# A routed feed-forward with LoRA conditioning, attention pooling and a quantised feed-forward: the first gather moved into the routing stage, slots and weights in a table of their own, copies of x spread, pooling loads moved up

## The chip, the cores and the metric

The kernel runs on one core of one Trainium2 chip. A core has TensorE (PE) for matmuls, VectorE (DVE), ScalarE (ACT) and GpSimd (POOL) for elementwise work, and SyncE (SP), which here only issues transfers. Each engine runs its own instruction stream, and they meet through semaphores. SP's transfers and POOL's run on the same 16 DMA engines, from two queues (q1 and q0 in the profile). The metric is the device time of one execution in microseconds, the median of several runs. One further execution is taken with the hardware profiler; all rows below are of that one.

## The reference

Eight batches of 512 tokens, 512 features, 4096 tokens in all. Cut to what matters:

```python
# stage 1: conditioning and routing. The experts see only the conditioned tensor c.
c = (x @ A[lang].T) @ B[lang].T + emb[lang]          # rank 16, 4 languages
vals, idx = top_k(c @ E.T, 2)                        # 8 experts, softmax over the two
caw = weights * (cumsum(weights > 0, axis=0) <= 512) # each expert keeps its first 512 tokens
tokens = c[index]                                    # 512 rows for each expert
out = relu(tokens @ w1[e].T) @ w2[e].T * vals        # inner width 1024
x = x + zeros.at[index].add(out)                     # scatter-add
# stage 2: attention pooling of x, then a feed-forward 512 -> 2048 -> 512 with
# row-quantised inputs (int8) and ternary weights, added to x
scores = tanh(x @ W1 + b1) @ v ; p = softmax(where(mask, scores, -1e30))
pooled = (p @ x) / count
out = x + bitlinear(gelu(bitlinear(pooled, w1, b1)), w2, b2)
```

c is never formed. It has rank 68 (64 LoRA coordinates and 4 language flags), so a token is a short row of features, and the first product of each expert is taken with G = (B, emb)-transposed times w1[e].

## The kernel before, in words

The program is four blocks one after another, with a barrier of all engines between them. At a block's end every engine executes a DRAIN and signals POOL, which releases all.

**Block 1, routing.** SP issues the small inputs, eight loads of the transposed x (`xt`, a ring of three), `w_in` of experts 0 to 2 and `w_raw` of expert 0, and then eight copies of x, 1 MB each, from the input to the DRAM tensor `x_after_experts` (x1), into which the experts add. For each batch PE makes the features (`feats`) and turns them; ACT keeps them in `feat` (`feat_cp`). The 32 tiles of 128 tokens are routed in two halves q. `choose(q)` on DVE finds the two best experts; the softmax needs one exponential on ACT, `exps(q)`. PE counts (`count`), and `give_slots(q)` on DVE gives each token its slot and writes one-hot rows: `tile_hot` for the slot's tile and `lane_hot` for its lane. There are 32 lane rows of 128 for a half: the 16 of the first choice are written by DVE, the 16 of the second by ACT (`hot_lanes`: 16 Abs and one Relu). `find(q)` on PE turns them into the token of each slot. After `find(1)`, DVE writes `row_of_slot`, the table of row numbers that every gather and scatter uses. POOL stores `feat`, 104 floats for each token: 100 features, then two slots and two weights. `expand(e, n)` makes half n of G for experts 0 and 1 in PSUM banks that are free; `high_g` (ACT) and `low_g` (DVE) split it into two parts for exact products.

**Block 2, experts.** POOL gathers the 512 rows of an expert in four indirect DMAs (`gather(e)`), two experts ahead, and scatters each expert's output with four indirect DMAs that add. PE first makes G of expert 2, then for each expert and each of eight steps k runs `inner_block` (two products) and `out_block` of the step before (twelve). `turn(e + 1)` transposes the next rows at k = 3. For experts e = 1 to 5, `expand(e + 2, k)` puts G of expert e + 2 between them. ACT and DVE split each inner result and each piece of the second weight (`w_h`, `w_l`); DVE computes the slots' weights at k = 3 (`weights(e)`). In experts 1 and 2 ACT also sums the absolute values of the feed-forward weights, from `raw`, which SP loads two buffers ahead; `take_y(e)` may write y only when the scatters of the expert before have landed (`y_out`).

**Block 3, pooling.** SP loads the masks and then `x_sum`, 1 MB for each batch, from x1, two ahead. Block 4 is the feed-forward.

## Time and profile before

| | before |
|---|---|
| median of 3 runs | 861.82 us (861.26 to 862.88) |
| the profiled execution's own time | 860.46 us |
| its span, first to last instruction | 858.7 us |
| mean granted TensorE clock | 0.94 |
| PE busy | 746.2 us, 87% |
| DVE busy / ACT busy / POOL busy | 498.7 / 503.8 / 312.8 us |

Busy time is the time in which an engine executed something; the span is that of the program's instructions. An idle stretch of an engine counts only where another engine could not go on without it.

### The profile page before, as it was taken

Reading aid. Unit: us, or ns where it says so; the run is one execution under the profiler, and the core shown is the slowest. Engines: PE = TensorE matmul, PEld = TensorE weight load, DVE = VectorE, ACT = ScalarE, POOL = GpSimd, SP = SyncE. Lnnn points to the kernel's source line nnn. Section 1 sums busy time; section 2 is a strip of 40 time slices with the busy share of each in tenths; the row PEclk is TensorE's granted clock in tenths of the full one; section 3 lists DMA queues with packets and bytes.
Section 4 is the critical chain, followed back from the end, with each engine's and each line's share of the span. In section 5 each row is a group of like instructions: output and inputs, shape, how many; then the busy total and the mean of one; then the engine's idle time right before and its main releaser. Section 6 shows DMA issues by size and latency. Waiting matters only on the chain. (4 is left out here: it accounts for less than half of the span.)

```text
span 858.7 us, 10173 instructions
## 1 busy us (share of the span) xinstructions
PE 746.2 (87%) x3504; PEld 474.8 (55%) x3504; DVE 498.7 (58%) x922; ACT 503.8 (59%) x714; POOL 312.8 (36%) x272
## 2 busy tenths in 40 slices
PE   6864899998999999444999999965699999999996
PEld 3322487776777777323677777754244444444442
DVE  2447354544555455123555555542689999999993
ACT  1144336663477688224566566542678888888883
POOL 0010324314233222204455545432145555555554
PEclk9987799999999999766999999978999999999999
DMA  7999449877467466331111102000112222222222
GB/s 234 372 398 337 136 176 343 276 270 241 162 150 175 178 148 147 49 130 50 49 50 50 44 14 92 1 1 1 37 50 74 74 69 69 73 74 73 74 65 72
DMA packets 40595, 109.00 MB, mean 127 GB/s; under 512 B 4320, under 2 KB 5104, under 8 KB 37344
## 3 DMA queue, kind: packets, MB, share of 16 engines
q1 hardware_dynamic: 33712, 94.84, 31.2%
q0 software_dynamic: 6320, 13.06, 8.2%
q8 instruction: 28, 0.46, 0.2%
q10 hardware_dynamic: 512, 0.45, 0.2%
q14 instruction: 23, 0.19, 0.1%
HBM read 88.59 MB, written 28.13 MB: 136 GB/s over the span
## 5 line engine op out<-in xcount | busy, mean ns | idle before, releaser
L1311 PE MATMUL ps<-ff_q,qt 128*128 128x512 bf16 x512 | 123.1, 385 | 4.6 <-PEq L949 3.1
L1335 PE MATMUL ps<-ff_q,ht 128*128 128x512 bf16 x512 | 118.0, 385 | 0.0
L846 PE MATMUL ps<-w_h,inner_l 128*128 128x512 f32 x256 | 102.8, 401 | 3.6 <-DVE inner_l L795 3.6
L848 PE MATMUL ps<-w_h,inner_h 128*128 128x512 f32 x256 | 101.2, 395 | 0.0
L847 PE MATMUL ps<-w_l,inner_h 128*128 128x512 f32 x256 | 101.2, 395 | 0.0
L661 POOL DMA_INDIRECT x_after_experts<-y,row_of_slot x32 | 51.5, 1609 | 134.6 <-DVE y L781 127.3
L1375 DVE SCALAR_TENSOR_TENSOR h<-ps,scale,bias 128x1024 f32<-128x1024 f32 x64 | 81.5, 1279 | 16.9 <-PE ps L1311 16.9
L730 ACT ACTIVATE inner_h<-ps 128x512 fp32r<-128x512 f32 x64 | 38.0, 594 | 81.5 <-PE ps L834 81.1
L1335 PEld LDWEIGHTS ps<-ff_q,ht 128*128 128x128 bf16 x512 | 50.7, 99 | 62.0 <-issue 3.5
L795 DVE SCALAR_TENSOR_TENSOR inner_l<-ps,inner_h 128x512 fp32r<-128x512 f32 x64 | 44.2, 690 | 70.1 <-ACT inner_h L730 69.6
L1354 ACT ACTIVATE h<-h,to_q 128x2048 int8<-128x2048 f32 x32 | 64.1, 2003 | 34.4 <-DVE to_q L1412 34.4
L1311 PEld LDWEIGHTS ps<-ff_q,qt 128*128 128x128 bf16 x512 | 49.3, 99 | 60.0 <-issue 6.5
L1380 DVE TENSOR_REDUCE mx<-h 128x1 f32<-128x1024 f32 x64 | 77.4, 1209 | 1.1 <-ACT h L1344 1.1
L1344 ACT ACTIVATE h<-h 128x1024 f32<-128x1024 f32 x64 | 67.1, 1049 | 16.0 <-DVE h L1375 16.0
L149 PE MATMUL ps<-w_in_sb,lora_b_sb 128*100 128x512 f32 x128 | 63.6, 619 | 9.1 <-PEq L225 9.1
L792 DVE TENSOR_TENSOR w_l<-w_raw,w_h 128x512 fp32r<-128x512 f32 x64 | 44.1, 690 | 45.2 <-ACT w_h L726 45.0
L1010 PE MATMUL ps<-x_h,prob_l 128*128 128x512 f32 x128 | 62.2, 486 | 8.0 <-ACT q L1097 8.0
L984 POOL TENSOR_TENSOR x_l<-x_sum,x_h 128x1024 fp32r<-128x1024 f32 x16 | 38.1, 2381 | 69.2 <-ACT x_h L1107 51.7
L1362 ACT ACTIVATE junk<-h 128x2048 bf16<-128x2048 f32 x32 | 61.1, 1911 | 1.0
L1291 POOL TENSOR_SCALAR ht<-hp 128x2048 bf16<-128x2048 int8 x32 | 60.8, 1901 | 1.2 <-DVE hp L1391 1.2
L846 PEld LDWEIGHTS ps<-w_h,inner_l 128*128 128x128 f32 x256 | 49.1, 192 | 15.2 <-DVE inner_l L795 4.9
L647 POOL DMA_INDIRECT rows<-token_features,row_of_slot x32 | 31.8, 993 | 65.9 <-DVE w_slot L766 47.3
(216 smaller groups left out, 1434.6 us busy)
## 6 DMA issues: line engine op xcount, KB each, us to landing
w_in_sb<-in_w_in_t SPq DMA_DIRECT2D x8, 2048.0 KB, 12.7
w_raw<-in_w_out_t SPq DMA_DIRECT2D x16, 1024.0 KB, 5.4
raw<-in_ff_t SPq DMA_DIRECT2D x16, 1024.0 KB, 7.5
xt<-in_x_t SPq DMA_DIRECT2D x8, 1024.0 KB, 8.9
x_after_experts<-in_x SPq DMA_DIRECT2D x8, 1024.0 KB, 18.5
x_sum<-x_after_experts SPq DMA_DIRECT2D x8, 1024.0 KB, 4.9
x<-x_after_experts SPq DMA_DIRECT2D x32, 256.0 KB, 2.7
out<-res SPq DMA_DIRECT2D x32, 256.0 KB, 2.0
```

Source lines behind the costliest of these rows:

```text
L149: return pe.matmul(ps[0:STACK_1, bank, :], lora_b_sb[:, k, :], w_in_sb[:, e % AHEAD, k, n * 512:(n + 1) * 512], start=k == 0, stop=k == KD ...
L846: pe.matmul(ps[:, s, :], inner_l[:, k % 2, c], w_h[:, k % RING, :], start=k == 0, stop=False)
L847: pe.matmul(ps[:, s, :], inner_h[:, k % 2, c], w_l[:, k % RING, :], start=False, stop=False)
L848: m = pe.matmul(ps[:, s, :], inner_h[:, k % 2, c], w_h[:, k % RING, :], start=False, stop=k == KI - 1)
L1010: pe.matmul(ps[:, NUM + j, :], prob_l[at_l], x_h[:, b % 2, l, :], start=first, stop=False)
L1311: m = pe.matmul(ps[:, f, :], qt[:, t, k, :], ff1_q[:, k, f * 512:(f + 1) * 512], start=k == 0, stop=k == KD - 1)
L1335: mm = pe.matmul(ps[:, OUT[t3 % 2], :], ht[:, t3 % 2, k // 2, k % 2, :], ff2_q[:, k, :], start=k == 0, stop=k == KF - 1)
L1344: act.activation(part, part, ACT.Gelu).then_inc(gelu, 1)
L1354: act.activation(h8[:, t1 % 2, :], h[:, t1 % 2, :], ACT.Copy, scale=to_q[:, t1 % 2:t1 % 2 + 1]).then_inc(h8_ready, 1)
L1362: act.activation(junk[:], h[:, t0 % 2, :], ACT.Square, accum_out=sq[:, t0 % 2:t0 % 2 + 1]).then_inc(h_sq, 1)
L1375: ve.scalar_tensor_tensor(h[:, t % 2, half], ff_bank[i], scale1[:, t:t + 1], bias1[:, half], ALU.mult, ALU.add).then_inc(biased, 1)
L1380: ve.tensor_reduce(mx[:, t % 2, i:i + 1], h[:, t % 2, i * HALF:(i + 1) * HALF], AX.X, ALU.max, apply_absolute_value=True).then_inc(h_max, 1)
```

## The change

It has five parts.

1. **exp and lane rows.** `exps(1)` on ACT stands inside `hot_lanes(0)`, after the Abs rows and ahead of the Relu. Four of the 16 second-choice lane rows of each half go from ACT to DVE. `count(1)` stands ahead of `expand(0, 1)`, and `find` is split in two, so that other products stand between.
2. **Own table.** Slots and weights go to a DRAM table of their own, `token_choices` (4 floats a token), with gathers of their own (`gather_choices`, four for each expert). `feat` can be stored as soon as the features are there.
3. **First gather.** `gather(0)` is issued at the end of block 1, after the semaphore `rows_known`. G of expert 2 is no longer made ahead of the experts: `expand`, `high_g` and `low_g` treat it like those of the later experts, inside expert 0.
4. **Copies of x.** Of the eight copies two stay in block 1, three are issued at the start of block 2, one in the middle and two near the end of expert 0. The `xt` loads are all ahead of `w_in`. The first scatter waits for all copies, where the gathers waited before.
5. **Pooling loads.** `x_sum` lives in the outer scope (its two buffers serve as two of the three `xt` buffers in block 1). SP waits for `y_out` in block 2 and issues the loads of batches 0 and 1 there. PE's wait for `setup` in block 3 stands at its first use.

```diff
-    feat_dram = nc.dram_tensor("token_features", [N_TOK + SPARE, ROW], F32, kind="Internal").ap()
+    feat_dram = nc.dram_tensor("token_features", [N_TOK + SPARE, STACK_1], F32, kind="Internal").ap()
+    choice_dram = nc.dram_tensor("token_choices", [N_TOK + SPARE, ROW - STACK_1], F32, kind="Internal").ap()
...
+        def copy_x(sp, b):
+
+            ts = slice(b * TPB, (b + 1) * TPB)
+            sp.dma_start(x1_v[:, ts, :], x_rows[:, ts, :]).then_inc(x1_init, DMA)
+
+        def load_x_sum(sp, b):
+            sp.dma_start(x_sum[b % 2][:], x1_v[:, b * TPB:(b + 1) * TPB, :]).then_inc(x_in[b % 2], DMA)
...
+
+        def gather(pool, e):
+
+            for s in range(SB):
+                pool.indirect_dma_start(
+                    rows[:, e % 2, s, :], None, feat_dram,
+                    bass.IndirectOffsetOnAxis(row_of_slot[:, e * SB + s:e * SB + s + 1], 0)).then_inc(rows_in[e % 2], DMA)
...
+                        for t in range(ACT_ROWS):
                             last = act.activation(lane_off[:, t, :], lane_id_b[:], ACT.Abs, bias=minus_lo[:, t:t + 1])
                         last.then_inc(lane_off_ready, 1)
+                        if q == 0:
+                            exps(1)
                         act.wait_ge(lane_off_ready, q + 1)
-                        act.activation(lane_hot[:, q % 2, QT:, :], lane_off, ACT.Relu, bias=1.0, scale=-1.0).then_inc(lanes_hot2, 1)
-
-                    def exps(q):
-                        act.wait_ge(gap_ready, q + 1)
-                        act.activation(gap_exp[:], gap[:], ACT.Exp).then_inc(exp_ready, 1)
+                        act.activation(lane_hot[:, q % 2, QT:QT + ACT_ROWS, :], lane_off[:, 0:ACT_ROWS, :], ACT.Relu, bias=1.0, scale=-1.0).then_inc(lanes_hot2, 1)
...
-                    exps(1)
+                    hot_lanes(1)
                     high_g(0, 1)
-                    hot_lanes(1)
...
-                    find(0)
+                    find(0, 0)
                     pe.wait_ge(lora_b_ready, 4)
                     pe.wait_ge(feat_t_cp, BATCH)
                     expand(0, 0)
+                    count(1)
+                    find(0, 1)
                     expand(0, 1)
-                    count(1)
                     expand(1, 0)
+                    find(1, 0)
+                    find(1, 1)
                     expand(1, 1)
-                    find(1)
...
+                        for t in range(ACT_ROWS, QT):
+                            hot = ve.tensor_scalar(lane_hot[:, q % 2, QT + t, :], lane_id_b[:], lo[:, 1, t:t + 1], None, ALU.is_equal)
+                        hot.then_inc(lanes_hot, 1)
+                        ve.tensor_copy(choice[:, here, 1::2].rearrange("p t k -> p k t"), slot[:]).then_inc(placed, 1)
                         ve.wait_ge(placed, q + 1)
...
-                    ve.scalar_tensor_tensor(row_of_slot[:], spare[:], -1.0, token[:], ALU.add, ALU.add)
+                    ve.scalar_tensor_tensor(row_of_slot[:], spare[:], -1.0, token[:], ALU.add, ALU.add).then_inc(rows_known, 1)
...
-                    for b in range(6):
+                    for b in range(BATCH):
                         load_x(b)
-                    load_w_in(0)
-                    for b in (6, 7):
-                        load_x(b)
-                    load_w_in(1)
-                    load_w_in(2)
+                    for e in range(AHEAD):
+                        load_w_in(e)
...
-                    for b in range(BATCH):
-                        ts = slice(b * TPB, (b + 1) * TPB)
-                        sp.dma_start(x1_rows[:, ts, :], x_rows[:, ts, :]).then_inc(x1_init, DMA)
+                    for b in (0, 1):
+                        copy_x(sp, b)
...
+                    pool.wait_ge(langs_ready, 1)
+
+                    def store_feats(q):
                         ts = slice(q * QT, (q + 1) * QT)
                         pool.wait_ge(feat_cp, PB * (q + 1))
+                        pool.dma_start(feat_v[:, ts, :], feat[:, ts, :]).then_inc(feat_out, DMA)
+
+                    def store_choices(q):
+                        ts = slice(q * QT, (q + 1) * QT)
                         pool.wait_ge(placed, q + 1)
-                        pool.dma_start(feat_v[:, ts, :], feat[:, ts, :]).then_inc(feat_out, DMA)
-                        if q == 0:
-                            pool.dma_start(spare_feat, zeros[:, 0:SB * ROW].rearrange("p (s f) -> p s f", s=SB)).then_inc(zero_out, DMA)
-                            for n in range(SB):
-                                pool.dma_start(x1_dram[N_TOK + n * P:N_TOK + (n + 1) * P, :], zeros[:]).then_inc(zero_out, DMA)
-                    pool.wait_ge(zero_out, DMA * (1 + SB))
+                        pool.dma_start(choice_v[:, ts, :], choice[:, ts, :]).then_inc(choice_out, DMA)
+
...
+                    store_feats(1)
+                    for q in range(PARTS):
+                        store_choices(q)
+                    pool.wait_ge(zero_out, DMA * (2 + SB))
                     pool.wait_ge(feat_out, DMA * PARTS)
+                    pool.wait_ge(rows_known, 1)
+                    gather(pool, 0)
...
-                    pe.wait_ge(w_in_in[AHEAD - 1], DMA)
-                    for n in (0, 1):
-                        for k in range(KD):
-                            m = g_product(pe, AHEAD - 1, n, k, n)
-                        m.then_inc(g_mm, 1)
                     turn(0)
...
-                            if 1 <= e <= EXPERTS - AHEAD:
+                            if e <= EXPERTS - AHEAD:
                                 expand(e + 2, k)
...
+                    sp.wait_ge(rows_in[0], DMA * SB)
+                    for b in (2, 3, 4):
+                        copy_x(sp, b)
                     sp.dma_start(w_in_sb[:, 0, :, :], w_in_v[AHEAD]).then_inc(w_in_in[0], DMA)
...
                             if e == 0:
                                 load_raw(i)
+                                for b in ((5,), (6, 7))[i]:
+                                    copy_x(sp, b)
...
+                    sp.wait_ge(y_out, DMA * SB * EXPERTS)
+                    for b in (0, 1):
+                        load_x_sum(sp, b)
 
...
+                    def gather_choices(e):
                         for s in range(SB):
                             pool.indirect_dma_start(
-                                rows[:, e % 2, s, :], None, feat_dram,
-                                bass.IndirectOffsetOnAxis(row_of_slot[:, e * SB + s:e * SB + s + 1], 0)).then_inc(rows_in[e % 2], DMA)
-
-                    gather(0)
-                    gather(1)
-                    pool.wait_ge(x1_init, DMA * BATCH)
+                                choices[:, e % 2, s, :], None, choice_dram,
+                                bass.IndirectOffsetOnAxis(row_of_slot[:, e * SB + s:e * SB + s + 1], 0)).then_inc(choices_in[e % 2], DMA)
+
+                    gather(pool, 1)
+                    pool.wait_ge(choice_out, DMA * PARTS)
+                    gather_choices(0)
+                    gather_choices(1)
                     for e in range(EXPERTS):
                         if e + 2 < EXPERTS:
-                            gather(e + 2)
+                            pool.wait_ge(rows_tr, e + 1)
+                            gather(pool, e + 2)
+                            pool.wait_ge(w_slot_ready, e + 1)
+                            gather_choices(e + 2)
                         for s in range(SB):
                             pool.wait_ge(y_cp[s % 2], e * SB // 2 + s // 2 + 1)
                             if s == 0 and e >= 1:
                                 pool.wait_ge(y_out, DMA * SB * e)
+                            if e == 0 and s == 0:
+                                pool.wait_ge(x1_init, DMA * BATCH)
...
-                        ve.wait_ge(rows_in[e % 2], DMA * SB * (e // 2 + 1))
+                        ve.wait_ge(choices_in[e % 2], DMA * SB * (e // 2 + 1))
...
                     sp.dma_start(mask[:], masks).then_inc(mask_in, DMA)
-                    for b in range(BATCH):
-                        if b >= 2:
-                            sp.wait_ge(x_trd, KD * (b - 1))
-                            sp.wait_ge(x_l_cp, 2 * (b - 1))
-                        sp.dma_start(x_sum[b % 2][:], x1_v[:, b * TPB:(b + 1) * TPB, :]).then_inc(x_in[b % 2], DMA)
+                    for b in range(2, BATCH):
+                        sp.wait_ge(x_trd, KD * (b - 1))
+                        sp.wait_ge(x_l_cp, 2 * (b - 1))
+                        load_x_sum(sp, b)
...
-                    pe.wait_ge(setup, 1)
...
+                            if b1 == 0:
+                                pe.wait_ge(setup, 1)
```

The order of instructions, at three places on which the prediction rests. ACT from its last feature copy to the second `hot_lanes`; `ff_q<-lane_id_b,minus_lo` is the Abs row, `ff_q<-ff_q` the Relu, `g<-ps` is `high_g`. Before:

```order
L313 ACTIVATE ff_q<-lane_id_b,minus_lo 128x128 x15
L316 ACTIVATE ff_q<-ff_q 128x2048 [waits lane_off_ready]
L325 ACTIVATE g<-ps 64x512 [waits g_mm]
L326 ACTIVATE g<-ps 100x512
L320 ACTIVATE gap_exp<-gap 128x16 [waits gap_ready]
L325 ACTIVATE g<-ps 64x512 [waits g_mm]
L326 ACTIVATE g<-ps 100x512
L313 ACTIVATE ff_q<-lane_id_b,minus_lo 128x128 [waits lanes_hot2,slot_ready]
```

and with the change:

```order
L355 ACTIVATE ff_q<-lane_id_b,minus_lo 128x128 x11
L348 ACTIVATE gap_exp<-gap 128x16 [waits gap_ready]
L360 ACTIVATE ff_q<-ff_q 128x1536 [waits lane_off_ready]
L365 ACTIVATE g<-ps 64x512 [waits g_mm]
L366 ACTIVATE g<-ps 100x512
L355 ACTIVATE ff_q<-lane_id_b,minus_lo 128x128 [waits lanes_hot2,slot_ready]
L355 ACTIVATE ff_q<-lane_id_b,minus_lo 128x128 x11
L360 ACTIVATE ff_q<-ff_q 128x1536 [waits lane_off_ready]
```

The exponential has moved from behind `high_g(0, 0)`, which waits for a product of PE, to behind twelve Abs rows. PE across the boundary of blocks 1 and 2, before; L397 is `find`, L149 a product of G, L826 `turn(0)`, L833 and L834 the first inner products:

```order
L397 MATMUL ps<-ff_q 128x64 x15
L225 UNCONDITIONAL_BRANCH
L819 UNCONDITIONAL_BRANCH [waits barrier_Pool_Activation_PE_DVE_SP_release]
L149 MATMUL ps<-w_in_sb,lora_b_sb 100x512 [waits w_in_in2]
L149 MATMUL ps<-w_in_sb,lora_b_sb 100x512 x7
L826 MATMUL ps<-const,rows 100x128 [waits rows_in0]
L826 MATMUL ps<-const,rows 100x128 x3
L833 MATMUL ps<-rows,g 128x512 [waits g_l_cp,rows_l_cp]
L834 MATMUL ps<-rows,g 128x512
```

and with the change (L439, L169, L880, L887, L888):

```order
L439 MATMUL ps<-ff_q 128x64 x15
L169 MATMUL ps<-w_in_sb,lora_b_sb 100x512 x4
L255 UNCONDITIONAL_BRANCH
L873 UNCONDITIONAL_BRANCH [waits barrier_Pool_Activation_PE_DVE_SP_release]
L880 MATMUL ps<-const,rows 100x128 [waits rows_in0]
L880 MATMUL ps<-const,rows 100x128 x3
L887 MATMUL ps<-rows,g 128x512 [waits g_l_cp,rows_l_cp]
L888 MATMUL ps<-rows,g 128x512
```

The eight products (16 records) of expert 2's G have left the place between the barrier and `turn(0)`; they are now dealt out over the steps of expert 0. POOL from its memsets to the first scatter, before:

```order
L271 DMA token_features<-feat 128x1664 [waits placed,feat_cp,zeroed]
L273 DMA token_features<-zeros 128x4x104
L275 DMA x_after_experts<-zeros 128x512 x4
L271 DMA token_features<-feat 128x1664 [waits placed,feat_cp]
L225 UNCONDITIONAL_BRANCH [waits feat_out,zero_out]
L638 UNCONDITIONAL_BRANCH [waits barrier_Pool_Activation_PE_DVE_SP_gather]
L647 DMA rows<-token_features,row_of_slot 128x104 [waits feat_out]
L647 DMA rows<-token_features,row_of_slot 128x104 x7
L647 DMA rows<-token_features,row_of_slot 128x104 [waits w_slot_ready,rows_tr,x1_init]
L647 DMA rows<-token_features,row_of_slot 128x104 x3
```

and with the change:

```order
L295 DMA token_features<-feat 128x1600 [waits feat_cp,langs_ready,zeroed]
L303 DMA token_features<-zeros 128x4x100
L305 DMA token_choices<-zeros 128x4x4
L308 DMA x_after_experts<-zeros 128x512 x4
L295 DMA token_features<-feat 128x1600 [waits feat_cp]
L300 DMA token_choices<-choice 128x64 [waits placed] x2
L175 DMA rows<-token_features,row_of_slot 128x100 [waits rows_known,feat_out,zero_out]
L175 DMA rows<-token_features,row_of_slot 128x100 x3
L255 UNCONDITIONAL_BRANCH
L695 UNCONDITIONAL_BRANCH [waits barrier_Pool_Activation_PE_DVE_SP_gather]
L175 DMA rows<-token_features,row_of_slot 128x100 x4
L699 DMA choices<-token_choices,row_of_slot 128x4 [waits choice_out]
```

Four gathers stand ahead of the branch that ends block 1 (`UNCONDITIONAL_BRANCH`, where the DRAIN stands in the trace), and eight gathers of choices follow behind the second four.

## Rows read from the trace of the kernel before

**Rows 1.** Two stretches: us, engines' busy time, granted clock, DMA share, GB/s.
```profile
0.00:85.45 85.45, 56.34 (x222) 24.30 (x222) 40.64 (x144) 27.75 (x65) 5.74 (x14) 0.88 0.94 336
...
352.85:374.88 22.03, 0.00 (x0) 0.03 (x1) 2.81 (x21) 0.69 (x1) 5.36 (x5) 0.56 0.62 144
```
**Rows 2.** Timeline of DVE: start, us, line, operation, [idle before <-releaser].
```profile
48.82 0.29 DVE L480 TENSOR_REDUCE best<-feat 128x16 f32<-128x128 f32 x1 [1.73 <-ACT feat L306]
...
62.30 0.17 DVE L492 TENSOR_SCALAR kept<-gap_exp 128x16 f32<-128x16 f32 x1 [9.86 <-ACT gap_exp L320]
...
71.40 2.69 DVE L535 TENSOR_SCALAR ff_q<-lane_id_b,slot_lo 128x128 bf16<-128x128 bf16 x16
...
77.03 0.19 DVE L551 SCALAR_TENSOR_TENSOR row_of_slot<-spare,token 128x32 uint32<-128x32 f32 x1
```
**Rows 3.** Timeline of ACT in the routing.
```profile
48.62 4.76 ACT L313 ACTIVATE ff_q<-lane_id_b,minus_lo 128x128 bf16<-128x128 bf16 x16
...
73.48 1.91 ACT L316 ACTIVATE ff_q<-ff_q 128x2048 bf16<-128x2048 bf16 x1
```
**Rows 4.** Timeline of PE, routing and the start of block 2.
```profile
38.04 5.30 PE L368 MATMUL ps<-xt,proj 128*72 128x512 f32 x8 [0.52 <-DMA xt<-in_x_t]
...
64.44 7.06 PE L149 MATMUL ps<-w_in_sb,lora_b_sb 128*100 128x512 f32 x16
...
75.44 1.00 PE L397 MATMUL ps<-ff_q 128*128 128x64 bf16 x16 [1.01 <-ACT ff_q L316]
...
85.49 8.90 PE L149 MATMUL ps<-w_in_sb,lora_b_sb 128*100 128x512 f32 x16 [9.05 <-PEq L225]
...
95.02 0.64 PE L826 MATMUL ps<-const,rows 128*100 128x128 f32 x4 [0.62 <-DMA rows<-token_features,row_of_slot]
```
**Rows 5.** Timeline of POOL: gathers of expert 0, first scatters of experts 0, 1, 6, 7.
```profile
86.20 1.05 POOL L647 DMA_INDIRECT rows<-token_features,row_of_slot  x1 [10.92 <-POOLq L225]
...
90.09 0.94 POOL L647 DMA_INDIRECT rows<-token_features,row_of_slot  x1 [0.30 <-issue]
...
128.56 1.63 POOL L661 DMA_INDIRECT x_after_experts<-y,row_of_slot  x1 [11.02 <-DVE y L781]
...
161.49 1.62 POOL L661 DMA_INDIRECT x_after_experts<-y,row_of_slot  x1 [15.40 <-DVE y L781]
...
326.65 1.56 POOL L661 DMA_INDIRECT x_after_experts<-y,row_of_slot  x1 [20.54 <-DVE y L781]
...
351.87 1.56 POOL L661 DMA_INDIRECT x_after_experts<-y,row_of_slot  x1 [18.05 <-DVE y L781]
```
**Rows 6.** POOL's DRAIN at the ends of blocks 1 and 2: ns, start us.
```profile
L225 POOLq DRAIN  x1: 645/645/645, 84.6 to 84.6; - x1
...
L608 POOLq DRAIN  x1: 5273/5273/5273, 363.1 to 363.1; - x1
```
**Rows 7.** Indirect gathers, minimum, median and maximum from issue to landing.
```profile
DMA to landing us min/median/max: 2.5/4.3/6.7
```
**Rows 8.** A stretch of copies and one of expert 1: columns as rows 1.
```profile
65.00:70.00 5.00, 5.00 (x13) 1.91 (x12) 4.59 (x15) 1.86 (x7) 0.00 (x0) 1.00 1.05 337
...
131.00:164.00 33.00, 33.00 (x134) 24.14 (x133) 15.89 (x26) 20.70 (x39) 10.54 (x9) 1.00 0.91 303
```
**Rows 9.** SP's issues at the end of expert 0, and the ACT operation that needs `raw` 2.
```profile
123.30 0.38 SPq L626 DMA_DIRECT2D w_raw<-in_w_out_t  x1
...
132.82 0.33 SPq L617 DMA_DIRECT2D raw<-in_ff_t  x1
...
144.44 1.05 ACT L699 ACTIVATE abs_junk<-raw 128x1024 int8<-128x1024 f32 x1
```
**Rows 10.** The boundary of blocks 2 and 3: last scatter, first pooling loads, first transposes.
```profile
357.46 1.56 POOL L661 DMA_INDIRECT x_after_experts<-y,row_of_slot  x1 [0.30 <-issue]
...
369.01 25.31 SPq L957 DMA_DIRECT2D x_sum<-x_after_experts  x3
...
374.88 1.94 PE L1042 MATMUL ps<-const,x_sum 128*128 128x128 f32 x8 [22.04 <-DMA x_sum<-x_after_experts]
```

119 lines of the change are left out of this document (62 added, 57 removed).

## The prediction

> **What bounds the kernel now.** First the stages. Block 1 takes 85.45 us, its DMA engines are busy 0.94 of it, and PE 56 us of it; between the last expert's product and the first transpose of the pooling lie 22.03 us with no matmul [rows 1]. In the experts PE is busy 33.00 of 33 us [rows 8]. So the change touches a stage bound by a chain of small steps, one bound by PE, and an empty stretch.
>
> In block 1 the reader is to see three waits in a row. DVE sits 9.86 us until 62.30 for one exponential of 16 columns [rows 2]: ACT had it behind `high_g(0, 0)`, and that behind a product of PE. Then the lane rows: DVE writes 16 in 2.69 us from 71.40, ACT's Relu ends at 73.48 + 1.91 = 75.39, and the last 16 products of `find` go from 75.44 to 76.44 [rows 2 to 4]. `row_of_slot` is there at 77.22. Last, PE turns the first gathered rows only at 95.02 [rows 4]: 17.8 us later, of which the barrier takes until 85.45 and the gathers the rest, with expert 2's G (8.90 us) made beside them.
>
> **Part 1, exp and lane rows.** `xt` 6 no longer stands behind `w_in` 0, whose wait was 0.52 us [rows 4], so ACT's lane rows start at 48.1 instead of 48.62. Twelve at 4.76/16 = 0.30 us end at 51.7 [rows 3]. DVE reaches the wait at 62.30 - 9.86 = 52.4, and 0.5 earlier now; four more rows of 0.17 us ahead of it hide in its wait of 1.73 us for features [rows 2]. So the exponential is ready when DVE comes, and the step at 62.30 stands at 52.05: 10.25 us earlier. In the second half the four rows are not hidden: DVE ends at 71.40 + 2.69 - 10.25 + 0.67 = 64.5. ACT ends at 75.39 - 10.25 less four Abs rows (1.2) and a quarter of the Relu (0.5), 63.5. The last half of `find` starts at 64.6 and not 75.44, 10.8 us earlier, and `row_of_slot` stands at 66.4. PE's share fits: between `count(1)` at 54.6 and 64.6 it has 16 products of `find` (1.0) and two halves of G, 7.06 us at the full clock and 8.90 when it starts at the lower one [rows 4]. At the longer price PE is there at 64.5, so that cover is thin.
>
> **Parts 2 and 3, the first gather.** The feature table is stored before the slots are known and is no longer waited for. POOL started its gathers 0.75 us after its release at 85.45, and three intervals took 90.09 - 86.20 = 3.89 us [rows 5]. From 66.4 the four run from 67.2 to 72.0, the last issued at 71.1. Its landing is bounded by 2.5 us [rows 7] and by 95.02 - 90.09 = 4.9 us under full DMA load [rows 4, 5]; the queue has nearly run empty by then, so I take 3.3: 74.4.
>
> What stands behind the gathers is the barrier, and it needs POOL's DRAIN. The trace has two: 0.65 us after plain transfers (block 1), 5.27 us after indirect ones (block 2), both begun when every transfer had landed [rows 6]. The new block 1 ends with indirect ones, so I take 5.27: the drain ends at 77.3, `turn(0)` starts at 77.6, 17.4 us before 95.02. With 0.65 the landing would set it, 74.6 or 20.4 us. DVE's `low_g` ends near 72.0 either way, hidden by POOL.
>
> Against this stands G of expert 2. Its 16 records cost 8.90 us where PE waited for the gathers anyway; in expert 0 PE is full, and they cost 7.06 us [rows 4]. Two scatters lie 32.93 us apart with an expansion between them and 25.22 us without one [rows 5], which bounds the price by 7.7; I take 7.1. Before, PE came to `turn(0)` from 8.9 busy microseconds; now from an idle stretch, as at 85.49, where the first four products took the lower clock. I add 0.7.
>
> The 32 gathers of choices are 1.3 us each on POOL. Those of expert 0 are issued by 88.6, land by 92, and are needed at k = 3, a little before the middle of the expert, about 95; later ones have some 15 us of POOL's idle time in each expert [rows 5]. They cost nothing; if one came late, DVE and PE would stand for that long.
>
> **Part 4, copies of x.** A copy moves 1.05 MB at 337 GB/s, 3.1 us of all engines [rows 8]. Two in block 1 end where they did, before the gathers. Three and `w_in` 3, 14.5 us of transfers, are done long before they are needed. The place to look is its end: 5.3 us before the first scatter (6.3 with the expansion) SP issues `w_raw`, `raw` 1, copies 6 and 7 and `w_in` 4: 2.6 + 2.6 + 6.2 + 5.2 us at 400 GB/s for loads, done 12 us after the first y is ready. `raw` 2, issued 4.3 us after it, is needed 15.9 us after it [rows 5, 9]. It lands between 15 and 21, the latter if the scatters take their full share in between. ACT stalls 0 to 5 us and PE has about one step in hand, 25.22/8 = 3.2 us, so the cost is 0 to 2, and 5 if nothing hides it. I take 1.5. The first scatter waits for copy 7 until about 9; y of expert 1 may be overwritten only from 33 on, so that wait is hidden.
>
> The Trainium skill (DMA: Bandwidth & Descriptors, section "Issuing engines are not separate DMA queues") says that transfers of all engines run on the same 16 DMA engines and interleave. The trace agrees: expert 1 shows a DMA share of 0.91 with loads from SP and scatters from POOL [rows 8]. By that rule the spread copies are not free time but moved load, which is the third rival below.
>
> **Part 5, pooling loads.** The last scatter is issued at 357.46; the drain begins at 363.1 [rows 6, 10], when all have landed. SP can issue the first load there, not at 369.01, and without the masks ahead of it. It was there 374.88 - 369.01 = 5.9 us after its issue behind the masks; alone I put it at 4.9, so at 368.0, inside POOL's drain, which ends at 368.4. PE starts its transposes at 368.8: 6.1 us saved. DVE's setup ends 3 us later, hidden by PE's first 8 us.
>
> **The sum**, against the profiled execution's own 860.46 us: -17.4 + 7.1 + 0.7 + 1.5 - 6.1 = -14.2, so 846.3; against the median of 861.82, 1.4 above it, 847.6. I say 847.5.
>
> **Rivals.**
> 1. *The drain grows with POOL's number of DMAs.* Block 1 has 7 of them for 0.65 us, block 2 has 64 for 5.27: 0.09 and 0.08 each. With 14 and 92 the drains would be 1.2 and 7.5 us. `turn(0)` then waits for the landing (20.4 saved), and the end saves 3.9 instead of 6.1: -20.4 + 9.3 - 3.9 = -15.0, 846.8. For it: the ratio. Against it: two points fit any line. If only plain DMAs' price held at the first boundary and 5.27 at the second, -17.2, 844.6.
> 2. *The drain reckons from the last indirect DMA.* In block 2 it ended 368.4 - 359.0 = 9.4 us after the last one was generated, in block 1 more than that after a plain one. From 72.0 that is 81.4: `turn(0)` 13.3 us earlier, -10.1 in all, 851.7.
> 3. *The copies' backlog reaches PE.* If nothing hides `raw` 2 to 4 coming late, 5 to 7 us instead of 1.5: 851 to 853. Against it: expert 1's buffers leave ACT 11.6 us for each [rows 9].
> 4. *Slower.* The drain costs 5.27 us for each of the gathers it follows, 21 us for four, so it ends at 93.1, `turn(0)` is 1.6 us earlier only, and with 9.3 of costs and the 6.1 at the end the kernel stands at 863.4. It decides from a drain of 19.5 us on; from 21.2 it is over 0.2% slower. Against it: 32 scatters and 28 gathers ahead of the other drain cost 5.27 together. That it ends just above 861.82 makes "slower" mean little more than no change.
>
> **How the numbers follow.** Forecast (fixed drain of about 5 us) 0.42; the drain by count or short 0.33; rival 2 0.10; rival 3 0.09; rival 4 or something unseen 0.06. The first two span 843.5 to 849.5 with the stall at 0 to 3.5; the range reaches to rivals 2 and 3 at 852. Faster by over 0.2% (1.7 us, about what a measurement of this kernel can tell from no change) 0.95, within it 0.03, slower 0.02.
>
> **What would show it.** DVE's wait for `gap_exp` under 0.5 us; `row_of_slot` near 66.4; POOL's first DRAIN 5 us, with the first transposes near 77.6; 95.02 to the first scatter, 33.5 us, growing to about 41; expert 1 within 2 us of 32.9; no wait of ACT for `raw`; 16 us between the last product of the experts and the first transpose of the pooling. I am wrong if the drain is 10 us or more, if `find` waits for PE's own G (cover of 0.1 us), or if expert 1 shows ACT waiting for `raw`.

## The result, and the profile after

| | before | changed | ratio |
|---|---|---|---|
| recorded result (4 runs each) | 862.35 us (861.26 to 863.36) | 848.74 us (843.28 to 850.21) | 0.9834 [0.9812, 0.9857] |
| first repeat (9 and 5 runs) | 862.93 us | 842.39 us (841.66 to 843.36) | 0.9763 [0.9742, 0.9784] |
| second repeat (10 and 6 runs) | 861.81 us | 840.82 us (838.96 to 843.69) | 0.9755 [0.9733, 0.9778] |

The recorded result lies 1.2 us above the forecast of 847.5. The two repeats lie under the forecast's range, and the forecast's terms have to be read against both: the profile of the recorded result holds a stall that the repeats don't show.

The stretches of the profile after, up to the first transposes of gathered rows, expert 0 and expert 1 (columns as [rows 1]):
```profile
0.00:75.69 75.69, 55.29 (x223) 23.80 (x223) 41.96 (x152) 24.49 (x57) 11.51 (x21) 0.97 0.87 305
75.69:122.39 46.70, 38.73 (x134) 27.15 (x135) 16.54 (x30) 13.26 (x24) 19.76 (x20) 0.86 0.65 228
122.39:155.61 33.22, 33.22 (x134) 24.00 (x133) 16.69 (x28) 21.40 (x40) 14.00 (x12) 1.00 0.92 307
```
The same three stretches in the profile of the first repeat:
```profile
0.00:74.95 74.95, 53.66 (x223) 22.92 (x223) 41.95 (x152) 24.46 (x57) 11.50 (x21) 0.99 0.89 308
74.95:113.69 38.74, 36.18 (x134) 25.76 (x135) 16.65 (x30) 13.37 (x24) 19.69 (x20) 0.89 0.79 275
113.69:146.89 33.20, 33.20 (x134) 24.02 (x133) 16.93 (x28) 21.50 (x41) 14.50 (x12) 1.00 0.95 321
```
The reader is to see that the first and the third agree within 1 us and that the whole difference of the two sessions, 8.0 us, sits in expert 0.

The routing chain after (timeline of ACT, DVE, PE and POOL; it answers to [rows 2 to 5]):
```profile
48.16 3.61 ACT L355 ACTIVATE ff_q<-lane_id_b,minus_lo 128x128 bf16<-128x128 bf16 x12
52.19 0.22 ACT L348 ACTIVATE gap_exp<-gap 128x16 f32<-128x16 f32 x1 [0.41 <-DVE gap L528]
...
53.36 0.17 DVE L538 TENSOR_SCALAR kept<-gap_exp 128x16 f32<-128x16 f32 x1
65.16 0.74 DVE L585 TENSOR_SCALAR ff_q<-lane_id_b,slot_lo 128x128 bf16<-128x128 bf16 x4
67.26 0.19 DVE L600 SCALAR_TENSOR_TENSOR row_of_slot<-spare,token 128x32 uint32<-128x32 f32 x1
...
68.35 1.05 POOL L175 DMA_INDIRECT rows<-token_features,row_of_slot  x1 [1.51 <-DVE row_of_slot L600]
72.23 0.95 POOL L175 DMA_INDIRECT rows<-token_features,row_of_slot  x1 [0.30 <-issue]
...
75.69 1.06 PE L880 MATMUL ps<-const,rows 128*100 128x128 f32 x4 [5.52 <-PEq L255]
```
DVE's wait of 9.86 us is gone, `row_of_slot` starts at 67.26 and not 77.03, and PE turns the first rows at 75.69 and not 95.02. POOL's DRAIN at the ends of blocks 1 and 2 (as [rows 6]):
```profile
L255 POOLq DRAIN  x1: 5899/5899/5899, 69.5 to 69.5; - x1
...
L657 POOLq DRAIN  x1: 4949/4949/4949, 359.3 to 359.3; - x1
```
The first now begins while POOL is still making the gathers, and ends at 75.4. The boundary of blocks 2 and 3 (as [rows 10]):
```profile
353.28 1.56 POOL L719 DMA_INDIRECT x_after_experts<-y,row_of_slot  x1 [0.30 <-issue]
...
359.12 0.82 SPq L147 DMA_DIRECT2D x_sum<-x_after_experts  x2
...
364.53 1.94 PE L1083 MATMUL ps<-const,x_sum 128*128 128x128 f32 x8 [16.06 <-PEq L657]
```
From the last scatter to the first transposes it is 11.25 us and was 17.42; PE's gap is 16.06 and was 22.04.

**The stall.** Of expert 0, the timeline of PE and ACT:
```profile
91.55 0.80 PE L887 MATMUL ps<-rows,g 128*128 128x512 f32 x1
92.19 0.40 PE L888 MATMUL ps<-rows,g 100*128 100x512 f32 x1
...
96.00 0.60 ACT L786 ACTIVATE inner_h<-ps 128x512 fp32r<-128x512 f32 x1 [6.35 <-remote]
...
104.61 0.60 ACT L786 ACTIVATE inner_h<-ps 128x512 fp32r<-128x512 f32 x1 [7.49 <-remote]
...
105.99 0.79 PE L898 MATMUL ps<-w_h,inner_l 128*128 128x512 f32 x1 [5.12 <-DVE inner_l L849]
```
ACT's `inner_h` waits for the product whose last part PE started at 92.19 and that is 0.40 us long; it ran at 96.00. The next product, started at 96.71, was read at 104.61. "Remote" means that a signal came but no instruction's end lies beside it. By the records of signals that there are, PE's came up to 8.0 us after their products, in order, until 104.8. PE itself ran on until it needed `inner_l`, and then sat 5.12 us; its products then took 0.63 us each and not 0.39, at the lower granted clock. In the repeat ACT read the same two products at 91.44 and 95.95, as PE gave them.

### The profile page after: what moved, and what is told of

It reads as the page before. It is cut to its first block and busy times, and to the rows that moved or that the text cites. A ratio compares the mean times of both kernels' runs of the same rounds, so it can differ in the third digit from the quotient of the medians.

```text
span 848.3 us, 10204 instructions
## 1 busy us (share of the span) xinstructions
PE 746.7 (88%) x3504; PEld 474.7 (56%) x3504; DVE 500.0 (59%) x930; ACT 500.4 (59%) x706; POOL 344.9 (41%) x307
## 5 line engine op out<-in xcount | busy, mean ns | idle before, releaser
L849 DVE SCALAR_TENSOR_TENSOR inner_l<-ps,inner_h 128x512 fp32r<-128x512 f32 x64 | 44.2, 690 | 79.7 <-ACT inner_h L786 66.6
L169 PE MATMUL ps<-w_in_sb,lora_b_sb 128*100 128x512 f32 x128 | 62.7, 603 | 0.0
L900 PEld LDWEIGHTS ps<-w_h,inner_h 128*128 128x128 f32 x256 | 49.3, 193 | 11.5
```

What stands on the lines that cost most here:

```text
L169: return pe.matmul(ps[0:STACK_1, bank, :], lora_b_sb[:, k, :], w_in_sb[:, e % AHEAD, k, n * 512:(n + 1) * 512], start=k == 0, stop=k == KD ...
L900: m = pe.matmul(ps[:, s, :], inner_h[:, k % 2, c], w_h[:, k % RING, :], start=False, stop=k == KI - 1)
```

## The experiments

Each was timed against the kernel before on its own chip; a kernel's ratio is to be read against 0.9763 and 0.9755 of the changed kernel. Experiments 2 and 3 and the first step of 4 ran beside the first repeat, experiment 8 and the first run of 7 beside the second. The others had only the kernel before beside them, so what they gained or lost is given by the ratios, as a range against the two repeats. All edits start from the changed kernel.

**1. The changed kernel again** (twice, no edit).

> The changed kernel once more, beside its variants on the same chip. Its first profile shows 46.7 us from the first transposes of expert 0 (75.69) to ACT's first y (122.39), of which ACT sat 6.35 us until inner_h at 96.00 and 7.49 us until inner_h at 104.61 although PE's products for them ended at 92.6 and 97.1, and PE then sat 5.12 us until 105.99. Its four times spread from 843.28 to 850.21. Theory: this stall comes in most executions and is what makes the time 848.7 and not 843: times between 843 and 850 again, with the two waits of ACT in the profile wherever the time is near 849. Rival: it was an accident of one execution; then the profile here has no such waits and the times lie within 2 us.

> The changed kernel a third time. Its first four times were 850.21, 849.70, 843.28 and 847.77, its five of the repeat 841.66 to 843.36. In the first profile ACT waited 13.84 us for signals of PE that came 3.4 to 8 us after the products had ended, and the trace misses many records of signals just in those stretches; in the profile of the repeat neither is seen, nor in any of its seven variants. If the stall belongs to the kernel (its full DMA engines at 77 to 102 us), some of the five are again above 846; if it belonged to that one session, all lie within 841 to 844 and expert 0 takes 38.7 us.

Measured: 842.39 and 840.82 us, and in both profiles no wait of ACT for "remote"; expert 0 takes 38.74 and 38.75 us. Their eleven times, 838.96 to 843.69, show none of it either. In the recorded session three of four times (847.77 to 850.21) lie where the stalled profile's does, so there it was no accident of one execution. Of the twelve profiles taken in these experiments one has it again (experiment 7).

**2. Copies 2, 3 and 4 later.**
```diff
-                    for b in (2, 3, 4):
-                        copy_x(sp, b)
...
                                 load_raw(i)
-                                for b in ((5,), (6, 7))[i]:
+                                if i == 0:
+                                    sp.wait_ge(w_l_cp, 6)
+                                for b in ((2, 3, 4, 5), (6, 7))[i]:
```


> Copies 2, 3 and 4 of x are issued with copy 5, after the sixth low half of w_out of expert 0 (near 106), where the DMA engines of the changed kernel are idle from 103 to 116; nothing else moves. Theory 1 (the copies keep the DMA engines full from 77 to 102 and PE's signals to ACT come late while they are): ACT starts inner_h(3) and inner_h(4) within 0.2 us of PE's product, expert 0 takes 40.5 to 41.5 us instead of 46.7, and the time falls by 5 to 6 us, to 842.5 to 844, with a spread under 2 us. Theory 2 (POOL's sixteen gathers one behind the other from 86.8 to 103.1 are the cause, whatever else the queue holds): no change, 848 to 850. Theory 3 (neither, an accident of the run): same times as the changed kernel on this chip.

Measured: 849.76 us (849.11 to 851.49), ratio 0.9842 [0.9821, 0.9863]: 7.4 us slower than the changed kernel, against all three theories. Expert 0 took 40.00 us, 1.3 more than in the repeat, so the rest lies behind it. The timeline of ACT in expert 1 says why (`rounded<-raw` is its sum of absolute values, which writes its unused result over the tile `rounded`), and below it stands the stretch of expert 1:
```profile
139.31 1.06 ACT L757 ACTIVATE rounded<-raw 128x1024 int8<-128x1024 f32 x1 [7.00 <-DMA raw<-in_ff_t]
...
150.71 1.06 ACT L757 ACTIVATE rounded<-raw 128x1024 int8<-128x1024 f32 x1 [6.13 <-DMA raw<-in_ff_t]
```
```profile
115.29:155.51 40.22, 36.42 (x134) 25.72 (x133) 16.37 (x27) 21.38 (x41) 14.29 (x12) 0.92 0.88 298
```
Two waits of ACT for `raw`, 13.1 us in all, make expert 1 7.0 us longer. That is the prediction's third rival with its own mechanism, in a variant where the copies come some 25 us later. In the three profiles of the changed kernel such waits add up to 1.9 to 3.7 us, as in the first repeat (us in total, times, longest):
```profile
ACT rounded L757 <- DMA raw<-in_ff_t: 1.9, 1, 1.9
```

**3. The gathers of choices later.**
```diff
                     gather_choices(0)
+                    pool.wait_ge(w_l_cp, 6)
                     gather_choices(1)
```


> POOL issues the four gathers of choices of expert 1, and the eight gathers for expert 2 behind them, only after the sixth low half of w_out of expert 0 (near 106); the copies stay where the changed kernel has them. Theory 1 (copies and full DMA engines): the two waits of ACT stay, the time is that of the changed kernel. Theory 2 (the row of small gathers): the waits are gone, expert 0 takes 40.5 to 41.5 us and the time falls by 5 to 6 us. If both variants cure it, it takes both together.

Measured: 841.75 us (840.01 to 845.02), ratio 0.9754 [0.9727, 0.9782], expert 0 38.7 us: no different from the repeat. The row of small gathers costs nothing, as the prediction had it; on the stall this says nothing, since the repeat beside it had none.

**4. Part 1 taken back, in two steps.** First the exponential alone; then PE's order with it.
```diff
-                        if q == 0:
-                            exps(1)
                         act.wait_ge(lane_off_ready, q + 1)
...
                     high_g(0, 0)
+                    exps(1)
```
```diff
                     find(0, 0)
+                    find(0, 1)
...
                     expand(0, 0)
+                    expand(0, 1)
                     count(1)
-                    find(0, 1)
-                    expand(0, 1)
                     expand(1, 0)
+                    expand(1, 1)
                     find(1, 0)
                     find(1, 1)
-                    expand(1, 1)
```


> The second exponential of the routing stands behind high_g(0, 0) again, as before the change; the lane rows shared with DVE and the split of find stay. Theory of the prediction (the place of the exponential was worth the whole wait of 9.86 us): DVE waits about 10 us again, row_of_slot comes 10 us later and the time rises by 9 to 10 us. Rival, read off the order: in the changed kernel PE makes G of expert 0 right behind the first half of find, at 49.1 to 52.8, so ACT's high_g(0, 0) could run at 53.7 to 54.7 and the exponential at 54.8, 2.5 us later only; then it was the split of find that freed it, DVE waits about 2.5 to 3 us and the time rises by 2.5 to 3 us.

> PE's order of block 1 and the place of the second exponential are those of before the change (find whole ahead of G, exponential behind high_g(0, 0)); lane rows stay shared 12 to 4, everything else as changed. With the exponential alone put back the time rose by 1.8 us and not by 10. If the split of find did the rest: DVE waits 7 to 10 us for the exponential, the first transposes come 7 to 10 us later and the time is 849 to 852 on this scale (ratio to before 0.985 to 0.988). Rival: a later row_of_slot is partly paid already by the landing of the gathers, which then meet an empty queue: 4 to 6 us only, 846 to 848.

Measured: 844.19 us, 1.8 slower than the repeat beside it; then 850.76 us, ratio 0.985 [0.9819, 0.988], 7.5 to 8.2 slower. The first transposes came at 77.50 and 83.72, 2.6 and 8.8 us later than in the first repeat. DVE's wait with the exponential put back alone, then with PE's order too, and PE in this last run:
```profile
54.99 0.18 DVE L537 TENSOR_SCALAR kept<-gap_exp 128x16 f32<-128x16 f32 x1 [2.46 <-ACT gap_exp L348]
```
```profile
61.58 0.17 DVE L537 TENSOR_SCALAR kept<-gap_exp 128x16 f32<-128x16 f32 x1 [9.45 <-ACT gap_exp L348]
```
```profile
53.48 1.04 PE L438 MATMUL ps<-ff_q 128*128 128x64 bf16 x16 [5.04 <-ACT ff_q L358]
54.33 9.36 PE L169 MATMUL ps<-w_in_sb,lora_b_sb 128*100 128x512 f32 x16
63.60 0.23 PE L423 MATMUL ps<-chosen,ones_b 128*128 128x136 bf16 x1
```
The wait of 9.86 us had two locks. ACT has the exponential behind `high_g(0, 0)`; and PE came to that product only after the second half of `find`, which waits for ACT's Relu. The new order of PE opens the second lock, and with it open the exponential's place is worth 2.46 us. The prediction credited all of it to the place. What in the new order does it is not separated, for the split of `find` and the place of `count(1)` were taken back together: PE's rows show `count(1)` at 63.60, right behind both halves of G, so in its old place it would have come no earlier even with the exponential early.

**5. The pooling's first loads back in block 3, and POOL's wait taken away.**
```diff
-                    sp.wait_ge(y_out, DMA * SB * EXPERTS)
-                    for b in (0, 1):
-                        load_x_sum(sp, b)
...
-                    for b in range(2, BATCH):
-                        sp.wait_ge(x_trd, KD * (b - 1))
-                        sp.wait_ge(x_l_cp, 2 * (b - 1))
+                    for b in range(BATCH):
+                        if b >= 2:
+                            sp.wait_ge(x_trd, KD * (b - 1))
+                            sp.wait_ge(x_l_cp, 2 * (b - 1))
```


> The first two loads of the pooling stand in the third block again, behind the masks; the rest as changed. Step of the prediction: 6.1 us slower than the changed kernel, 848 to 849 (ratio 0.983), with 22 us and not 16 between the last product of the experts and the first transpose. Rival: the gap is set by POOL's drain of 4.95 us alone, since PE's first transpose follows its end by 0.3 us in the changed kernel: then the loads' place is worth only the part beyond the drain, and without the masks' contention less than 6: 2 to 4 us.

```diff
-                    pool.wait_ge(y_out, DMA * SB * EXPERTS)
```


> POOL does not wait for the landing of the last scatters before its drain in block 2 (SP still does before it loads x_sum). In block 1 the drain began while the gathers were under way and ended 0.62 us after the last had landed, in four profiles; in block 2 it began when all had landed and took 4.95 us. If a drain of scatters costs about 5 us from its beginning whatever has landed: it begins near 355.5 and ends near 360.5 in place of 364.3, PE then waits only for x_sum, landed 364.0: 0.3 to 0.5 us faster. If it costs 5 us from the last landing on: no change in its end, none in the time. If it ends 0.6 us after the landing as in block 1: 359.8, and the same 0.3 to 0.5 us.

Measured: loads back, 846.09 us (845.55 to 848.80), ratio 0.9809 [0.9784, 0.9834], 4.0 to 4.7 us slower. Its profile:
```profile
356.46 0.90 SPq L147 DMA_DIRECT2D x_sum<-x_after_experts  x2
...
362.23 1.97 PE L1081 MATMUL ps<-const,x_sum 128*128 128x128 f32 x8 [22.07 <-DMA x_sum<-x_after_experts]
```
PE's gap is 22.07 us again, 5.6 more than the repeat's 16.48, and PE follows the load and not the barrier. The profile bears out the step's size; the times, with intervals of some 2 us on each side, don't contradict it. Without POOL's wait the time is 842.30 us, ratio 0.9751 [0.9723, 0.9779], no different from the changed kernel, and its DRAIN is this:
```profile
L657 POOLq DRAIN  x1: 13692/13692/13692, 343.1 to 343.1; - x1
```
It ends at 356.8, 3.8 us after the last scatter's landing (issued 347.15, 5.9 us to landing) and not 4.95 + 0.2 as when it is held back until then. PE no longer follows the barrier but the load, whose landing it meets.

**6. G of expert 2 in the holes of block 1.**
```diff
                     expand(0, 0)
+                    expand(0, 1, range(0, 2))
                     count(1)
...
-                    expand(0, 1)
+                    expand(0, 1, range(2, KD))
                     expand(1, 0)
+                    expand(1, 1, range(0, 2))
...
-                    expand(1, 1)
+                    expand(1, 1, range(2, KD))
+                    pe.wait_ge(feat_cp, BATCH)
+                    expand(2, 0)
+                    pe.wait_ge(rows_known, 1)
+                    expand(2, 1)
...
-                            if e <= EXPERTS - AHEAD:
+                            if 1 <= e <= EXPERTS - AHEAD:
                                 expand(e + 2, k)
```
`expand(2, 1)` writes the bank that `find` used, which is the bank of G in block 2; ACT and DVE take it there as they do now.

> G of expert 2 leaves expert 0 and is made in block 1, in the holes that PE has there in the changed kernel (2.60 us before count(1), 6.02 us before the first transposes in its repeat); parts of the other halves are moved forward so that it fits. Theory of the sum (the growth of expert 0 from 32.7 to 38.7 us is G's products on a full PE): expert 0 takes 32 to 33 us, the first transposes stay within 0.5 us of 74.95, and the kernel is 6 to 7 us faster than the changed kernel: ratio to before about 0.969, 835 to 836 us. Rival A (block 1 has no such hole: ACT's and DVE's halves of G or PE itself come after POOL's drain): the first transposes stand 1.5 to 2.5 us later, gain 4 to 5. Rival B (expert 0 is paced by ACT, DVE or w_in and not by PE's products): expert 0 stays near 38 us and nothing is gained.

Measured: 835.75 us (834.69 to 836.76), ratio 0.9684 [0.966, 0.9708], 6.1 to 6.8 us faster than the changed kernel. PE at the boundary, and the stretches of experts 0 and 1:
```profile
65.86 8.81 PE L169 MATMUL ps<-w_in_sb,lora_b_sb 128*100 128x512 f32 x20
75.03 0.62 PE L889 MATMUL ps<-const,rows 128*100 128x128 f32 x4 [0.36 <-PEq L255]
```
```profile
75.03:107.29 32.26, 29.60 (x118) 23.09 (x119) 15.06 (x28) 12.41 (x22) 18.92 (x20) 0.89 0.89 305
107.29:141.62 34.33, 33.47 (x134) 23.94 (x133) 16.47 (x27) 21.38 (x41) 14.47 (x12) 1.00 0.94 319
```
The transposes stand where they stood, PE has filled its 6 us, and expert 0 is 6.5 us shorter. Of that, 1.1 us goes again in expert 1.

**7. All eight copies of x in block 1,** and the same with the four small loads ahead of them.
```diff
-                    for b in (0, 1):
+                    for b in range(BATCH):
                         copy_x(sp, b)
...
-                    for b in (2, 3, 4):
-                        copy_x(sp, b)
...
-                                for b in ((5,), (6, 7))[i]:
-                                    copy_x(sp, b)
```


> All eight copies of x are issued in block 1 again, before the loads for pooling, as before the change; own tables, the gather in block 1 and the rest stay. Theory 1 (the gathers share the 16 DMA engines with the copies but have their own queue, so they land 6 to 7 us after their issue and not 3): POOL's drain ends near 79; SP's own issues, which stand on a full queue until about 81 as before the change, then end the block at 81.7, so the first transposes come 6 to 7 us later than 74.95, and without the later backlog expert 1 loses 0.3 us less: 848 to 849, ratio 0.983. Theory 2 (the gathers wait for all bytes queued ahead of them): they land at 88 or later, first transposes near 89, 856 to 857, ratio 0.993. Theory 3 (copies ahead are harmless): under 1 us.

> As with all eight copies in block 1 (852.77 us, first transposes at 87.88), but SP issues the four small loads for the pooling ahead of the copies. There SP's copies held it from 35.32 to 80.90 and the four small issues until 87.49, while the last gather had landed at 82.69 and POOL's drain had ended at 83.32. Theory 1 (SP's issues, not the landing of the gathers, ended the block): SP is done near 81 to 82, POOL's drain decides, first transposes at 83.5 to 84, 4 us faster: 848.5 to 849 (ratio 0.985). Theory 2 (the full DMA engines decide, and a gather's landing moves with them): the gathers land later and the time stays within 1 us of 852.8.

Measured: 852.77 us (849.75 to 855.82), ratio 0.9895 [0.987, 0.9921], 12 us slower than the repeat beside it and outside all three theories. SP's issues and the DRAINs of block 1:
```profile
35.32 45.58 SPq L144 DMA_DIRECT2D x_after_experts<-in_x  x8
80.94 4.57 SPq L279 DMA_DIRECT2D kind_i<-in_kind  x1
...
86.83 0.60 SPq L282 DMA_DIRECT2D att_w_sb<-in_att_w  x1
```
```profile
L255 POOLq DRAIN  x1: 14702/14702/14702, 68.6 to 68.6; - x1
...
L255 SPq DRAIN  x1: 122/122/122, 87.5 to 87.5; - x1
```
And how long the four gathers of that block took to land, minimum, median, maximum:
```profile
DMA to landing us min/median/max: 6.3/6.7/11.4
```
SP, not POOL, ends the block: it stands on its own issues until 87.5, while POOL's DRAIN ended at 83.3. Both are late: the gathers land 6.3 to 11.4 us after their issue, against 3.0 to 4.9 in the first repeat and 2.5 to 3.4 in the profile with the exponential put back. With the small loads first, the transposes came at 79.55, 8.3 us earlier than at 87.88. So SP's issues had ended the block, as theory 1 has it; but it put the transposes at 83.5 to 84, and the gathers, which had landed at 82.7, now landed at 78.1, with POOL's DRAIN ending at 78.8 and SP's at 79.3. Yet the time is 853.25 us (850.10 to 855.29), ratio 0.989 [0.9863, 0.9916], for expert 0 was 45.48 us long. Its stretch, and one product of PE with ACT's read of it:
```profile
79.55:125.03 45.48, 39.72 (x134) 28.20 (x135) 16.44 (x30) 13.24 (x24) 19.98 (x20) 0.81 0.62 219
```
```profile
96.21 0.40 PE L884 MATMUL ps<-rows,g 100*128 100x512 f32 x1
...
102.92 0.60 ACT L782 ACTIVATE inner_h<-ps 128x512 fp32r<-128x512 f32 x1 [9.26 <-remote]
```
ACT read the product 6.3 us after it had ended. That is the stall of the recorded profile once more. It cost 6.5 us here against the 39.0 us of expert 0 in the run before; without it this execution's 854.31 us would be 847.8, below all six times, so the others probably had part of it too.

**8. What the runs pointed to.** Experiment 6, with `w_in` of experts 4 to 7 issued after the `raw` loads of the following expert's first half, and without POOL's wait.
```diff
                             if inside(2 * (e - 4) + i, 6):
                                 load_raw(10 + 2 * (e - 4) + i)
-                        if e + AHEAD + 1 < EXPERTS:
-                            n = e + AHEAD + 1
+                            if i == 1 or e == 0 or e + AHEAD >= EXPERTS:
+                                continue
+                            n = e + AHEAD
```


> G of expert 2 in block 1, as measured at 835.75 us; w_in of experts 4 to 7 is issued after the raw loads of the following expert's first half, so that raw 2 and 3 don't stand behind its 5 us; and POOL has no wait for the last scatters. If the 1.1 us by which expert 1 was longer there (34.33 against 33.20 us) came from raw standing behind w_in 4: expert 1 takes 33.0 to 33.3, ACT waits under 2 us for raw, and with 0.4 us at the end the time is 1 to 1.5 us lower, 834.3 to 835 (ratio 0.967). Rival: the bytes queued ahead matter and not their order, or w_in itself comes late for G: no gain, or up to 3 us lost in expert 2.

Measured: 834.44 us (831.92 to 835.90), ratio 0.968 [0.9657, 0.9704]; the changed kernel beside it 840.82. Expert 1:
```profile
107.58:140.81 33.23, 33.23 (x134) 24.01 (x133) 17.02 (x28) 21.61 (x41) 14.72 (x12) 1.00 1.01 346
```
ACT has no wait for `raw` left and expert 1 is back at 33.23 us. So the 1.1 us of experiment 6 came from `raw` standing behind `w_in` 4. This kernel is 6.4 us faster than the changed one beside it, and nearly all of that is experiment 6; that it is also faster than experiment 6, by 1.3 us in the medians, is not shown, since their intervals overlap.

## Why the prediction was right, and where it was not

The terms, read off the first y of ACT (before: 127.73 for expert 0, 351.57 for expert 7; recorded 122.39 and 347.20; repeat 113.69 and 338.52) and the first transposes:

| term, us | forecast | recorded profile | first repeat |
|---|---|---|---|
| first transposes earlier | -17.4 | -19.3 | -20.1 |
| expert 0 longer (G, lower clock) | +7.8 | +14.0 | +6.0 |
| experts 1 to 7 (forecast: late `raw`) | +1.5 | +1.0 | +1.0 |
| end of the experts to the pooling | -6.1 | -6.0 | -5.6 |
| the rest | 0 | +0.1 | -0.2 |
| sum against 860.46 | -14.2 | -10.2 | -18.8 |

**The recorded number was met in part by accident.** Against the repeat each term is within 2.7 us, and the mechanisms were right except for that of the first drain, the share of the exponential and the cost of late `raw`. But the recorded 848.74 contains a stall of some 8 us that no step of the prediction has; without it the kernel stands at 841 to 842, below the range that the prediction gave. What put the forecast 5 to 7 us above that are mainly three terms mis-sized on the same side: the drain (2.7), G (1.8) and experts 1 to 7 (0.5).

**The drain.** The prediction took 5.27 us from 72.0, where POOL has made its last gather, although both drains that it had read began only when everything had landed; by that reading it should have counted from its own landing at 74.4, and would have come to 79.7. What the runs show is that in block 1 POOL's DRAIN runs beside the gathers and ends 0.62 to 0.63 us after the last has landed, in all thirteen profiles. In the first repeat (the last gather, its time to landing, the DRAIN):
```profile
71.00 0.94 POOL L175 DMA_INDIRECT rows<-token_features,row_of_slot  x1 [0.30 <-issue]
...
DMA to landing us min/median/max: 3.0/3.0/3.0
...
L255 POOLq DRAIN  x1: 6389/6389/6389, 68.3 to 68.3; - x1
```
The last gather has landed at 74.04 and the DRAIN ends at 74.67. In the run with the exponential put back these are 76.59 and 77.22, and with all copies in block 1 82.69 and 83.32, so the DRAIN moves with the landing. That is the case which the prediction named beside its choice ("with 0.65 the landing would set it", 20.4 us) and made half of its first rival. The other half, growth by count, is wrong: block 2's DRAIN is 4.95 us after 92 transfers and was 5.27 after 64. The DRAIN's length, 5.9 and 6.4 us, comes near the 5 us that the prediction named as a sign, but only because it begins early. Rivals 2 and 4, which put its end at 81.4 and 93.1, are out as well. Why a drain of landed scatters takes 5 us stays open.

**G.** PE's busy time in expert 0 grew by 36.18 - 29.06 = 7.12 us, the 7.1 of the sum. The stretch grew by 6.0 only, because 1.1 us of PE's idle time fell away (2.56 in the repeat, 3.65 before, whose row is this):
```profile
95.02:127.73 32.71, 29.06 (x118) 23.25 (x119) 16.34 (x28) 12.91 (x25) 5.08 (x5) 0.90 0.30 106
```
The 0.7 for a lower clock is not seen on top: the mean granted clock of the stretch is 0.89 against 0.90, and the busy time has grown by the 7.1 alone. Experiment 6 shows that expert 0 gets 6.5 us shorter when G leaves it.

**Late `raw`.** The sum had 1.5 us for it, and "expert 1 shows ACT waiting for `raw`" was named as a sign of being wrong. ACT did wait, 1.9 to 3.7 us in all, and no cost of it shows: from first y to first y expert 1 takes 33.20 to 33.22 us in the three profiles of the changed kernel, and 33.19 and 33.22 in two that have no such wait (all copies in block 1; experiment 8). The +1.0 of the table is something else. It is spread over all seven stretches, each 0.1 to 0.3 us longer than before, although the first repeat has its only wait for `raw` in expert 1; its cause stays open.

**Part 1.** 10.2 us were forecast for the exponential, with `row_of_slot` ready at 66.4; it was ready at 67.45 in the recorded profile and 66.22 in the repeat. The size was right and its cause incomplete: PE's new order carries most of it (experiment 4). The four lane rows, the order of the `xt` loads and the own table were not run alone.

**Copies.** The prediction costed them as a burden only, 1.5 us, and of the early gather it said only that the queue would be nearly empty by then, without a price for the opposite. Experiment 7 shows it: left in block 1 they take back 12 of the 20 us, by SP's own issues first. The Trainium skill (DMA: Bandwidth & Descriptors, section "Issuing engines are not separate DMA queues") says that transfers of all issuing engines interleave on the same 16 DMA engines; the trace agrees for the gathers, which land in 6.3 to 11.4 us with all eight copies ahead of them and in 3.0 to 4.9 with two. The part of SP standing on its issues is seen in its row of 45.58 us.

**The end.** As forecast, within 0.5 us.

**What stays open** is the stall. The recorded profile has it, and one of the twelve taken in the experiments. Their DMA share is that of profiles without it (from 80 to 102 us 1.00 in the recorded one, 0.98 in the repeat), so full DMA engines alone don't make it. Both profiles that have it, and only they, lack records of signals: of `in_mm`'s 65 the recorded profile holds 59 and the other 61. But the records are lacking far beyond the stall, of ACT's and DVE's signals too, and until about 280 us, while experts 1 to 7 took 224.81 us in the recorded profile and 224.83 in the repeat; lost records alone don't slow the kernel. The Trainium skill (NOTIFIC — the notification-queue block, section "7.1 Overflow: three behaviours, one of which stalls the engine") says that when the ring of trace records is full, new records are dropped, old ones are overwritten or the engine that makes them is stalled, depending on its settings. By that rule the stall could belong to the recording and not to the kernel. The trace fits it only in part: records are lost, but that is another of the page's three cases than a stalled engine, and PE was not held, for its products ran on and only its signals came late. No run here was made without recording, so this is a lead and not shown.

## What to carry to other kernels

When a wait is freed, look for a second lock behind it: the engine that releases may itself stand behind what the waiting one makes. When a chain of small steps gets shorter, count the holes that it leaves on the busy engine, and move work into them from the stretch that this engine bounds; here that was worth nearly a third of what the change gave. Bulk transfers without a due time are neither free early nor late: put before a dependent gather they delay its landing and hold the issuing queue, and put too late they push the next loads past their users.

## What was unexpected of the hardware

- POOL's DRAIN behind indirect gathers ended 0.62 to 0.63 us after their landing, in thirteen profiles. Behind scatters that had landed it took 4.95 us, and ended 3.8 us after their landing when it was already waiting.
- SP stood 45.58 us on the issues of eight transfers of 1 MB each while the DMA engines were full (share 1.04 from 60 to 76 us), and 4.57 us on a small load behind them.
- In two profiles ACT read products of PE up to 7.5 and 6.3 us after they had ended, while PE went on. Why is open.
